# A graph layer with a gated update: edge bias to VectorE, a sum to GpSimd, the store and its waits moved

## The reference

```python
h = maximum(layernorm(x), 0)
for t in range(4):
    m = relu(concat(h[src], h[dst]) @ W1[t] + b1[t]) @ W2[t] + b2[t]
    msgs += where(edge_type == t, m, 0)
agg = segment_sum(msgs, dst)
gi, gh = agg @ W_ih.T + b_ih, h @ W_hh.T + b_hh
r, z = sigmoid(i_r + h_r), sigmoid(i_z + h_z)
n = tanh(i_n + r * h_n)
out = x + (1 - z) * n + z * h
```

## Time and profile before

| | us |
|---|---|
| median of three executions | 1738.05 (1735.42 to 1740.06) |
| the profiled execution | 1735.05 |
| its span, first to last instruction | 1733.2 |
| PE busy (matmul) | 1616.9 (93%) |
| DVE (VectorE) busy | 1629.0 (94%) |
| ACT (ScalarE) busy | 1458.7 (84%) |
| POOL (GpSimd) busy | 1003.4 (58%) |

### The profile page before, as it was taken

How to read it: one execution, slowest core, us unless ns; L and a number is a source line. 1 busy time by engine, 2 the same in 40 slices (tenths; PEclk the granted TensorE clock), 3 DMA queues, 4 the chain that set the end, 5 groups by cost and what they waited for, 6 DMA issues and landing times. The chain is left out here.

```text
span 1733.2 us, 43005 instructions
## 1 busy us (share of the span) xinstructions
PE 1616.9 (93%) x10182; PEld 1421.4 (82%) x10182; DVE 1629.0 (94%) x4752; ACT 1458.7 (84%) x3404; POOL 1003.4 (58%) x1325
## 2 busy tenths in 40 slices
PE   0337999999999999999999999999999999999998
PEld 0326888888888888888888888888888888888887
DVE  8987999999999999999999999999999999999986
ACT  0126999999999999999999999999999999999896
POOL 5755656666666666655555555565655555555500
PEclk9956999999999999999999999999999999999999
DMA  2235777777777777777777777777777777777653
GB/s 84 70 87 154 193 195 206 203 200 200 203 200 203 199 199 203 198 200 196 199 198 200 200 195 201 196 200 195 197 201 194 201 196 199 197 196 200 188 143 100
DMA packets 477080, 320.07 MB, mean 185 GB/s; under 512 B 105917, under 2 KB 463117, under 8 KB 476974
## 3 DMA queue, kind: packets, MB, share of 16 engines
q10 hardware_dynamic: 261792, 156.12, 29.3%
q1 hardware_dynamic: 186638, 107.42, 25.5%
q0 software_dynamic: 28544, 55.41, 13.1%
HBM read 212.08 MB, written 107.07 MB: 184 GB/s over the span
## 5 line engine op out<-in xcount | busy, mean ns | idle before, releaser
L613 POOL DMA_INDIRECT e_x<-in_x,rows_now x816 | 824.4, 1010 | 248.4 <-issue 239.0
L1258 ACT ACTIVATE e_h<-e_x,shift,rstd 128x128 f32<-128x128 f32 x816 | 355.8, 486 | 90.0 <-DVE shift L1114 57.0
L1275 ACT ACTIVATE n_h<-n_x,shift,rstd 128x128 f32<-128x128 f32 x784 | 385.3, 492 | 2.9 <-issue 2.9
L1414 PE MATMUL bank<-n_h_hi,whh_hi 128*128 128x512 f32 x588 | 249.2, 424 | 1.2 <-ACT n_zc L1366 1.2
L1414 PE MATMUL bank<-n_a_hi,wih_hi 128*128 128x512 f32 x588 | 246.4, 419 | 0.9 <-DVE bank L1154 0.9
L1494 PE MATMUL bank<-n_sel,n_win 128*128 128x256 f32 x1568 | 234.7, 292 | 0.4 <-DVE n_sel L1142 0.4
L1416 PE MATMUL bank<-n_a_hi,wih_lo 128*128 128x512 f32 x588 | 232.5, 395 | 0.0
L1416 PE MATMUL bank<-n_h_hi,whh_lo 128*128 128x512 f32 x588 | 231.7, 394 | 0.0
L1415 PE MATMUL bank<-n_h_lo,whh_hi 128*128 128x512 f32 x588 | 231.2, 393 | 0.0
L1142 DVE TENSOR_SCALAR n_sel<-iota,n_rel 128x256 fp32r<-128x256 f32 x784 | 229.6, 357 | 0.1
L1415 PE MATMUL bank<-n_a_lo,wih_hi 128*128 128x512 f32 x588 | 229.6, 391 | 0.0
(11 more groups left out here) (193 smaller groups left out, 3812.4 us busy)
## 6 DMA issues: line engine op xcount, KB each, us to landing
n_win<-messages SPq DMA_DIRECT2D x1568, 64.2 KB
messages<-e_msg ACTq DMA_DIRECT2D x204, 257.0 KB, 2.9
n_x<-in_x ACTq DMA_DIRECT2D x195, 256.0 KB
out<-n_out ACTq DMA_DIRECT2D x195, 256.0 KB
e_x<-in_x,rows_now POOLq DMA_INDIRECT x816
rows_now<-lists SPq DMA_DIRECT2D x204, 2.0 KB
lists<-picks,list_rows POOLq DMA_INDIRECT x54, 2.8
w<-in_W SPq DMA_DIRECT2D x1, 512.0 KB, 5.0
```

The source lines that it names most:

```text
L613: G.indirect_dma_start(e_x[:, s, 2 * end + t, :], None, x, bass.IndirectOffsetOnAxis(ap=rows_now[:, s, t, end:end + 1], axis=0)).then_inc( ...
L1258: last = A.activation(e_h[:, s % 2, k, :], e_x[:, s, k, :], ACT.Relu, scale=rstd[:, slot, col + k:col + k + 1], bias=shift[:, slot, col + ...
L1275: last = A.activation(n_h[:, s % 2, cols], n_x[:, s, cols], ACT.Relu, scale=rstd[:, slot, col + 4 + k:col + 5 + k], bias=shift[:, slot, co ...
L1414: T.matmul(o, w_hi, v_hi, start=start, stop=False, skip_group_check=onto)
```

## The change

Five things are changed:

1. The bias matmul L1518 goes; each L1522 product starts its own accumulation. The biased message is made by VectorE: PSUM plus `b2_two` (b2 on all partitions, in a buffer of its own now) into the place of the low half, at the end of step i for unit i-9 (`e_biased`). TensorE's next first product waits for `e_biased` instead of `e_low`.
2. The high half is ScalarE's copy of that, from SBUF, one step later, behind the first two edge tiles and ahead of `n_r`. The low half subtracts it in place, both from SBUF, behind `n_sel` instead of ahead of it.
3. `n_xh` is added by GpSimd between its two pairs of gathers; VectorE's `n_out` waits for it.
4. The store stands behind the second pair of edge tiles (in the first 16 steps at the step's end).
5. SyncE's window loads are ordered by pairs of types, and in even steps each pair waits for the store of the unit of its own types; in odd steps there is no wait.

```diff
@@ SyncE
-                    else:
-                        q, qs = g + AHEAD, (m - LAG + 2 + AHEAD) % UNROLL
-                        sp.wait_ge(e_stored[qs], uses(q, qs, UNROLL, 16))
...
-                    for half in range(2):
-                        for t in range(TYPES):
+                    for pair_ in range(2):
+                        if m % 2 == 0:
+                            q = g + AHEAD - 1 + pair_
+                            if not isinstance(g, int):
+                                qs = (m - LAG + 2 + AHEAD - 1 + pair_) % UNROLL
+                                sp.wait_ge(e_stored[qs], uses(q, qs, UNROLL, 16))
...
+                        for half in range(2):
+                            for t in (2 * pair_, 2 * pair_ + 1):
@@ GpSimd
+            def node_sum(g, m):
...
+                pool.wait_ge(n_normed, g + 1)
+                if due(g - 3):
+                    pool.wait_ge(n_outed, g - 3)
+                G.tensor_tensor(n_xh[:, s % 4, :], n_h[:, s % 2, :], n_x[:, s, :], ALU.add).then_inc(n_xhed, 1)
...
                     relative_tags(i - LAG + 1, m - LAG + 1)
+                node_sum(i - LAG + 1, m - LAG + 1)
                 if within(i, UNITS):
                     gather(i, m, (1,))
@@ VectorE
                     dve.wait_ge(e_high, q + 1)
-                    V.tensor_tensor(e_msg[:, s, :, D:2 * D],
-                                    bank[BE1][:, message_part].rearrange("p (t d) -> p t d", t=2),
+                    V.tensor_tensor(e_msg[:, s, :, D:2 * D], e_msg[:, s, :, D:2 * D].bitcast(F32),
                                     e_msg[:, s, :, 0:D].bitcast(F32), ALU.subtract).then_inc(e_low, 1)
...
                     dve.wait_ge(n_back, g + 1)
+                    dve.wait_ge(n_xhed, g + 1)
...
-                    dve.wait_ge(n_normed, g + 1)
-                    V.tensor_tensor(n_xh[:, s % 4, :], n_h[:, s % 2, :], n_x[:, s, :], ALU.add).then_inc(n_xhed, 1)
...
+            def biased(i, m):
+                q, s = i - 9, (m - 9) % UNROLL
+                if within(q, UNITS):
+                    dve.wait_ge(e_messaged, q + 1)
+                    first = 2 * ((m - 9) % 2)
+                    V.tensor_tensor(e_msg[:, s, :, D:2 * D].bitcast(F32),
+                                    bank[BE1][:, message_part].rearrange("p (t d) -> p t d", t=2),
+                                    b2_two[:, first * D:(first + 2) * D].rearrange("p (t d) -> p t d", t=2),
+                                    ALU.add).then_inc(e_biased, 1)
@@ ScalarE
                 normalise_edges(i, m, (0, 1))
+                q, s = i - 10, (m - 10) % UNROLL
+                if within(q, UNITS):
+                    act.wait_ge(e_biased, q + 1)
+                    act.wait_ge(e_tagged, q + 1)
+                    A.activation(e_msg[:, s, :, 0:D], e_msg[:, s, :, D:2 * D].bitcast(F32), ACT.Copy).then_inc(e_high, 1)
...
-                store_messages(i, m)
                 normalise_edges(i, m, (2, 3))
+                in_head = isinstance(i, int) and i < LAG - 2
+                if not in_head:
+                    store_messages(i, m)
...
-                q, s = i - 9, (m - 9) % UNROLL
-                if within(q, UNITS):
-                    act.wait_ge(e_messaged, q + 1)
-                    act.wait_ge(e_tagged, q + 1)
-                    A.activation(e_msg[:, s, :, 0:D], bank[BE1][:, message_part].rearrange("p (t d) -> p t d", t=2),
-                                 ACT.Copy).then_inc(e_high, 1)
@@ TensorE
-                        pe.wait_ge(e_low, q)
+                        pe.wait_ge(e_biased, q)
...
-                    T.matmul(bank[BE1][:, message_part], ones_r[:], b2_rows[:, first * D:(first + 2) * D],
-                             start=True, stop=False)
...
-                        last = T.matmul(o, e_r[:, s, t * P:(t + 1) * P], w2[:, first + t, :], start=False, stop=t == 1)
+                        last = T.matmul(o, e_r[:, s, t * P:(t + 1) * P], w2[:, first + t, :], start=True, stop=True)
```

## The result

The changed kernel takes 1970.64 us, the kernel before 1736.74 on the same chip: 1.1346 times as long, 95% interval 1.133 to 1.1362. I had forecast 1819, at most 1872. The direction was right; the loss is 234 us, not 81. One of the four executions of the changed kernel took 3275 us, for a reason that the record does not show, while the other three took 1967.83 to 1971.25.

The account below looks back on a forecast made before the run. The prediction took the loop gate z, `n_zc`, `n_e`, `n_out`, gate `h_n` as the bound, with a mean room of 0.06 us. 1735 + 52 (bias) + 29 (late `n_sel`) = 1816, 1819 against the median; range 1772 to 1872.

Parts of the forecast that it names:

- Bias on the loop: VectorE's bias lengthens the loop gate z, `n_zc`, `n_e`, `n_out`, gate `h_n` by 0.27 us a step, 52 us.
- Late low half: GpSimd's sum delays `n_sel`, so low half, store and `e_ht` on ScalarE come late for TensorE: 29 us.
- Sum by GpSimd: Taking `n_xh` off VectorE gains 0, as VectorE idles there instead; on GpSimd the sum takes 1.2 us.
- It fits by volume: GpSimd, busy 4.7 of 8 us a step, has room for the sum.
- The rival with the sum ahead on the loop: In one step of four the sum precedes a layer norm operation between `n_e` and bias: 53 us more, 1872; chance 0.22.
- SyncE 0: SyncE's new waits for stores ahead of its loads cost 0, hidden by a step of cover ahead of `n_sel`.
- The bias matmul worth 0: Dropping it saves TensorE 0.12 us a step, but gate r then waits for `n_zc`: gain 0, at most 0.06.
- the high half 0: ScalarE's copy ahead of `n_r` costs 0, held by 0.38 us idle there and the place freed behind `n_h`.
- the start 0: Up to 160 us, 12 biases add 4 us on VectorE and ScalarE halts less: 0, from -4 to +4.

Follow-up runs that it names:

- u_low: The changed kernel with the sum back on VectorE and the low half back ahead of `n_sel`; 1790.70 us, 1.0317.
- u_ln: The changed kernel with the layer norm operation that VectorE did behind `n_e` moved ahead of `n_e`; 1905.30 us, 1.0975.
- p_ln: The kernel before with the sum on GpSimd and the layer norm operation moved ahead of `n_e`; 1814.48 us, 1.0462.
- p_sp: The kernel before with SyncE's part of the change alone: waits for stores in even steps, by pairs of window loads; 1730.84 us, 0.9978.
- u_sum: The changed kernel with the sum of normalised rows and x back on VectorE; 1817.64 us, 1.0468.
- p_late2: The kernel before with the sum on GpSimd ahead of the gathers, for the group of the step before, released by `n_ted`; 1816.67 us, 1.0475.

## Why the prediction was wrong, point by point

- *Bias on the loop, 52 us (41 to 64)*: 55, by u_low. The step and the size fit: 0.33 more from `n_e` to `n_out`, and a mean step of 8.27 us against 7.99, where I had 0.27 more. That all 55 us are the bias is argued, not shown.
- *Late low half, 29 us (0 to 62)*: the number came near by luck, the reason did not hold. I took the loss of `n_sel` through the sum and measured the room at TensorE's L1505. Without any sum the place of the low half costs 27 us, because ScalarE, which issues the store, halts ahead of `e_ht`, does not catch up until `n_n`, and `n_n`, `n_d`, `n_e` are the loop again. I had asked when `e_ht` was wanted, not how much idle time ScalarE had behind it.
- *Sum by GpSimd, 0 of its own*: this is the step that failed. It costs 153 us in the changed kernel, 166 alone. The size was nearly right: I took 1.2 us, with the end 1.04 behind `n_e`; it is 1.28 where it meets no `n_e`, and it ends 1.15 behind `n_e`. What I had wrong is the order and the path. I let the sum touch only `n_sel`, off the loop, and put VectorE's next operation ahead of it; in its place the runs show the sum ahead of the layer norm operation on the loop, which then takes some 1.27 us instead of under 0.2 (65 us by u_ln, 86 by p_ln). "It fits by volume" holds in the mean and not in the step behind the writes of lists, which takes 10.8 or 12.4 us in p_ln where the others take 8.08, seventeen times.
- *The rival with the sum ahead on the loop (0.22, 53 us more)*: this is what happened, larger. I counted one step of four, since I let only operations with two SBUF inputs be locked out; L1121, a one-input operation, is held just as long wherever it meets the sum, in 30 of its 48 steps, so that 78 steps are held, 85 us. What I put against it, that VectorE's next operation starts 0.08 before `n_e` ends, was no protection: in the second step shown it starts so, and takes 1.26 us. The Trainium skill (SBUF — State Buffer, section SBUF: two separate sides) says that the one that starts first keeps the shared pair of ports for its whole instruction, against a VectorE operation in a two-port mode as well as against one with two SBUF inputs; the 1.26 us of L1121 and the 1.38 us of the cast agree with a hold for the whole instruction, and I had named that half of the rule without using it. Which came first can't be read from the records: the cast's starts 0.04 before the sum's and is held all the same. No run shows the mode of an operation.
- *SyncE 0*: right by p_sp, which is if anything some 5 us faster; it was not tried inside the changed kernel.
- *The bias matmul worth 0, the high half 0, the start 0*: no run takes one of them alone. That u_low's 55 us leave no gain in sight fits the first, but does not show it.
- *Sum of the parts*: 55 + 27 + 153 = 235 us, which adds up because each was measured on top of the last. Of the 153, u_ln separates 65 for the lock on the loop. Of the other 88, the steps of u_ln put some 33 into the 18 that take 10.27 us behind the writes of lists (8.41 in u_sum) and some 50 into all others (8.72 against 8.41). What holds these others, a longer `n_sel` or ScalarE's halts, was not separated.

## What to carry to other kernels

Before work goes to GpSimd, lay its whole length, from the moment its input is ready, over VectorE's queue, and look there for arithmetic and casts that read and write SBUF, however small: here one of 32 columns that stood on a loop was held for what was left of the sum, 1.1 us. Check the room of a late result on the engine that waits for it, not only at the consumer behind that engine. And size a queue by its fullest step, here the one behind the writes of lists, not by its mean.

## What was not expected of the hardware

A VectorE operation of 0.18 us (32 columns, one SBUF input) takes 1.26 us beside a GpSimd sum, 1.08 of it held; a cast of two columns takes 1.38 us. Operations from PSUM and one SBUF tile keep their length beside the sum (bias 0.42, `n_out` 0.68), and so do two of the statistics, which read SBUF alone, in p_late2 (0.77 us for the pair, as without the sum):

```profile
881.61 1.28 POOL L679 TENSOR_TENSOR n_xh<-n_h,n_x 128x512 f32<-128x512 f32 x1
...
882.11 0.77 DVE L1061 BATCH_NORM_STATS2 bn<-n_x 128x6 f32<-128x256 f32 x2
```

GpSimd's 128x512 sum takes 1.28 to 1.29 us; where its record shows 1.57 to 1.61, it begins inside `n_e` and holds the wait for it. The Trainium skill's ratio (GPSIMD Engine Reference, section Elementwise, side-by-side cycle accounting) gave an estimate of 1.34 us; the measured 1.29 is close.
